# Unread full-array products in a Perceiver block's temperature network: eight ahead of its second layer in every other slot, thirteen behind its third

## What is computed

```python
qk = jnp.einsum('bhqd,bhkd->bhqk', Q, K)
scores = qk / math.sqrt(dk)
mean_sim = scores.mean(axis=(-2, -1))
max_sim = scores.max(axis=-1).mean(axis=-1)
probs = jax.nn.softmax(scores, axis=-1)
entropy_proxy = jnp.var(probs, axis=-1, ddof=1).mean(axis=-1)
feats = jnp.stack([mean_sim, max_sim, entropy_proxy], axis=-1)
hidden = jax.nn.gelu(_linear(feats, w1, b1), approximate=False)
hidden = jax.nn.gelu(_linear(hidden, w2, b2), approximate=False)
log_t = jnp.clip(_linear(hidden, w3, b3), LOG_T_MIN, LOG_T_MAX)
t = jnp.exp(log_t)[..., None]
attn = jax.nn.softmax(qk / (2.0 * t), axis=-1)
out = jnp.einsum('bhqk,bhkd->bhqd', attn, V)
```

## Time and profile before

| | |
|---|---|
| runs | 1214.53, 1217.95 and 1223.5 us, median 1217.95 |
| span of the profiled execution | 1213.1 us |
| TensorE products busy | 1101.5 us (91%) |
| VectorE, ScalarE, GpSimd busy | 812.4, 765.5 and 406.0 us |
| mean granted clock of TensorE | 0.897 |

### The profile page before, as it was taken

How to read it: one execution, slowest core, us unless ns; L and a number is a source line. 1 busy time by engine, 2 the same in 40 slices (tenths; PEclk the granted TensorE clock), 3 DMA queues, 4 the chain that set the end, 5 groups by cost and what they waited for, 6 DMA issues and landing times.

```text
span 1213.1 us, 39205 instructions
## 1 busy us (share of the span) xinstructions
PE 1101.5 (91%) x14964; PEld 892.8 (74%) x14964; DVE 812.4 (67%) x2128; ACT 765.5 (63%) x1547; POOL 406.0 (33%) x420
## 2 busy tenths in 40 slices
PE   3867799999999999999999999999999999999864
PEld 3535587878888787878878797878787887867743
DVE  4467667566776776677777776577667777578245
ACT  2434576776766676767766776667767676766521
POOL 2268352223232331433232332333143233331223
PEclk9968798987979897989999898989889898989787
DMA  4610010201010111102010111102020100000000
GB/s 132 193 29 27 23 37 4 61 11 42 19 44 21 36 29 28 37 2 54 11 45 20 37 29 29 36 4 61 2 54 11 45 20 19 3 2 6 8 2 9
DMA packets 46812, 38.85 MB, mean 32 GB/s; under 512 B 14576, under 2 KB 46000, under 8 KB 46640
## 3 DMA queue, kind: packets, MB, share of 16 engines
q1 hardware_dynamic: 46640, 36.41, 11.1%
HBM read 34.30 MB, written 2.10 MB: 30 GB/s over the span
## 4 chain that ended last, share of the span: by engine, by line
PE 75%; DVE 12%; issue 5%; ACT 4%; DMA 2%; POOL 1%; SPq 1%; DVEq 0%; ACTq 0%; POOLq 0%
PE pjp L665 14%; PE s1p L704 14%; PE s2p L735 13%; PE pjp L658 12%; PE pvp L752 8%; DVE est L1392 3%; DVE negm L1386 2%; PE tlp L848 2%; PE tlp L866 1%; PE tlp L787 1%; ACT ering L1045 1%; PE tlp L842 1%; PE s2p L725 1%; PE s2p L645 1%; PE tlp L809 1%
## 5 line engine op out<-in xcount | busy, mean ns | idle before, releaser
L1386 DVE TENSOR_REDUCE negm<-s1p 128x1 f32<-128x400 f32 (+1 forms) x512 | 289.8, 566 | 199.1 <-PE s1p L704 196.6
L1045 ACT ACTIVATE ering<-s1p,negm 128x400 f32<-128x400 f32 (+1 forms) x512 | 303.8, 597 | 118.6 <-DVE negm L1386 112.2
L1056 ACT ACTIVATE pring<-s2p 128x512 f32<-128x512 f32 x427 | 240.8, 565 | 148.1 <-PE s2p L735 145.1
L704 PE MATMUL s1p<-kt,qbd 32*128 32x400 f32 (+1 forms) x1024 | 305.2, 608 | 28.1 <-ACT ering L1045 26.1
L1392 DVE BATCH_NORM_STATS2 est<-ering 128x6 f32<-128x400 f32 (+1 forms) x512 | 290.7, 568 | 19.6 <-ACT ering L1045 19.6
L735 PE MATMUL s2p<-q2bd,kt 32*128 32x128 f32 (+1 forms) x3192 | 244.6, 285 | 0.0
L735 PEld LDWEIGHTS s2p<-q2bd,kt 32*128 32x128 f32 (+1 forms) x3192 | 233.3, 194 | 5.8
L658 PE MATMUL pjp<-cr,wkv 128*128 128x256 f32 (+1 forms) x1344 | 192.4, 295 | 29.7 <-DVE vt L1358 19.2
L1264 POOL TENSOR_TENSOR cr<-stage,cr 128x512 fp32r<-128x512 f32 (+1 forms) x112 | 132.1, 1180 | 234.3 <-ACT cr L1036 234.3
L658 PEld LDWEIGHTS pjp<-cr,wkv 128*128 128x128 f32 x1344 | 171.8, 198 | 45.5 <-issue 29.1
L665 PE MATMUL pjp<-wkv,cr 128*128 128x256 f32 (+1 forms) x1200 | 195.7, 318 | 10.0 <-ACT kt L1018 9.8
(11 more groups left out here) (278 smaller groups left out, 1033.1 us busy)
## 6 DMA issues: line engine op xcount, KB each, us to landing
stage<-in_ctx SPq DMA_DIRECT2D x96, 256.0 KB, 3.0
qbd<-q_dram SPq DMA_DIRECT2D x128, 8.0 KB, 1.8
stage<-in_ctx SPq DMA_DIRECT2D x16, 65.0 KB, 2.5
vt<-in_x SPq DMA_DIRECT2D x1, 1024.0 KB, 6.8
q_dram<-late SPq DMA_DIRECT2D x1, 1024.0 KB, 4.6
late<-in_x SPq DMA_DIRECT2D x7, 128.0 KB, 2.3
out_y<-late SPq DMA_DIRECT2D x7, 128.0 KB, 1.8
late<-in_gate SPq DMA_DIRECT2D x1, 768.0 KB, 4.9
```

The lines of the kernel that those rows point to most:

```text
L704: nc.tensor.matmul(s1p[u % 3][:, 0:w], qbd[s.par][rows, g, :], kt[s.par][rows, g, lo:lo + w], start=True, stop=True).then_inc(s1_full, 1)
L1045: nc.scalar.activation(ering[:, u % 3, 0:w], s1p[u % 3][:, 0:w], ACT.Exp, bias=negm[s.par][:, p, c:c + 1]).then_inc(s1_exp, 1)
L1056: nc.scalar.activation(ring_place(s, v)[0:m, 0:n], s2_bank(s, v)[0:m, 0:n], ACT.Exp).then_inc(s2_exp, 1)
L1386: nc.vector.tensor_reduce(negm[s.par][:, p, ch:ch + 1], s1p[u % 3][:, 0:w], AX.X, ALU.max, negate=True).then_inc(s1_max, 1)
```

## The change

A new function, `keep_clock(s, n, at)`, issues n products of 128 by 128 by 256 on TensorE, with the projection weights as both operands and the bank of the second-score unit of step `at` (8, thus unit 24 of the batch before) as target. Nothing reads them, and no semaphore counts them: unit 24's first product starts the bank afresh. Ahead of them TensorE waits until ScalarE has read that bank (`s2_exp`), the wait that unit 24 has anyway. It is called in step 6 ahead of the network's second layer, with n = 8 in odd slots and n = 0 in even ones (the wait alone), and in step 7 behind the third layer, with n = 13 in every slot. Both calls need a batch before with second scores, so they issue nothing in slot 1 and run in slots 2 to 16: 7 x 8 + 15 x 13 = 251 products.

```diff
@@ -79,6 +79,10 @@
 MLP_AT = {5: 0, 6: 1, 7: 2}
+
+
+FILL_FOR = 8
+FILL_1, FILL_2 = {1: 8, 2: 0}, 13
 N_MLP = len(MLP_AT)
@@ -666,6 +670,14 @@
                 mm.then_inc(pj_full, 1)
+
+            def keep_clock(s, n, at):
+                s_, v = s.second(at, 0)
+                if s_.has(1, B) and not s_.drains():
+                    need(pe, s2_exp, s_.lin(S2U, v - 1 - S2U))
+                    for _ in range(n):
+                        nc.tensor.matmul(s2_bank(s_, v)[:, 0:D], wkv[:, 0, 0, 0, 0:P], wkv[:, 1, 0, 0, :], start=True,
+                                         stop=True)
 
             def temperature(s, n):
@@ -885,6 +897,7 @@
                         if step in MLP_AT and s.has(1, B):
+                            keep_clock(s, FILL_1[s.r], FILL_FOR)
                             temperature(s, MLP_AT[step])
@@ -897,6 +910,8 @@
                     if step % 2 == 1 and step in MLP_AT and s.has(1, B):
                         temperature(s, MLP_AT[step])
+                        if MLP_AT[step] == 2:
+                            keep_clock(s, FILL_2, FILL_FOR)
```

## The result

The changed kernel takes 1200.96 us (median of 4 runs, 1197.27 to 1205.8), the kernel before 1216.51 beside it: a ratio of 0.985 (95% interval 0.981 to 0.990). In a second comparison, against 19 runs of the kernel before, it was 0.989 (0.986 to 0.992). So it is faster by 1.1 to 1.5%, the way that was forecast, at half the size: 13 to 16 us where 30 were expected. All ratios leave out two slow runs, one of the experiment `quarter` (1276.81 us at a mean clock of 0.77) and one of the kernel before (1229.07 us).

The account below looks back on a forecast made before the run. TensorE, busy 91% of the span and often at half clock, was taken as the bound. Gains 36.3 - 5.5 - 5 + 4.2 = 30.0 us off 1213.1 gave 1183.1, plus 4.85 to the median: 1188 us, range 1172 to 1210.

Parts of the forecast that it names:

- only the odd slots hold: Rival, chance 0.13: even slots' first fall may move to steps 10 to 13 and cost the same; 12.4 us gained, 1205.5.
- its own case: The forecast, chance 0.60: products hold the clock in most of slots 2 to 15; 1188 us, alone spanning 1176 to 1203.
- the price of 0.21: Lower bound, from whole odd slots: 0.21 us gained per low microsecond of the whole first stretch; 0.41 of busy time was taken.
- The first low stretch: Half-clock stretch behind the network, slots 2 to 15: removal gains 2.3 us per odd slot, 2.6 per even, 36.3 in all.
- two slots that fall as before: Of the 14 slots 2 to 15, two were allowed to keep their fall: 5 us lost.
- Steps 8 and 9: Sign of being right: from first scores to the end of the twelve projection products, 5.5 us before, near 3.3 after.
- The even slots' second fall: Later low stretch in seven even slots, no product added there: up to 0.80 us a slot, 0.6 taken, 4.2 us gained.
- the array theory: On TensorE, stretches in which little of the array works, not idling alone, precede a fall of the clock.
- The thirteen: Products behind the third layer: 0.25 us overrun by 14 slots, 3.5 us; in slot 16 3.2 us, of which 2 taken.
- the eight: Products ahead of the second layer in seven odd slots: 1.11 us in a gap of 1.13, costing nothing.
- the distance to the median: The median of the runs put 4.85 us above the profiled span, so 1183.1 became 1188.
- The rule that the prediction cited: Mid-kernel drops follow long idle gaps; products would then close nothing that matters, as in the unchanged-clock rival: 1225 us, chance 0.11.

Follow-up runs that it names:

- quarter: The changed kernel with the same 251 products on 32 contraction rows in place of 128: 1220.67 us, 1.001 of the kernel before.
- Whole tiles: The changed kernel with the last context tile's projections streaming 256 columns for 66 and 128 weight columns for 65: 1184.49 us, 0.971 of the kernel before.
- trim: The changed kernel with whole last context tiles, and eleven products behind the third layer in place of thirteen: 1189.11 us, 0.973 of the kernel before.
- no16: The changed kernel with whole last context tiles, without the thirteen products in slot 16: 1186.92 us, 0.973 of the kernel before.
- the clip moved: The kernel before with VectorE's clip of the network's output moved ahead of step 8's first maximum: 1218.54 us, 1.003 of the kernel before.
- wide_only: The kernel before, without added products, with the last context tile's projections streaming whole tiles: 1212.81 us, 0.993 of the kernel before.

## Why the prediction was right, and where it was too large

The time lies in the range, the sign is right, and the mechanism is shown: full-array products in the gaps hold the clock (the changed kernel), products of a quarter of the array in the same gaps do not (quarter, even slots). The size is half of the forecast: 1200.96 and 1204.31 us are nearer to the 1205.5 of the rival "only the odd slots hold" than to 1188, at the weak end of what the prediction worked out for its own case (15 us of gain, 1203, with the price of 0.21). Each term can be looked up.

*The first low stretch, 36.3 us, less 5 us for two slots that fall as before.* It went in 13 of 14 slots and is halved in slot 2, so no slot had to be given up. Steps 8 and 9 take 3.13 to 3.15 us from slot 3 on, where 3.3 were expected. What failed is the price carried over to the whole slot. An odd slot gained 65.49 - 64.18 = 1.3 us (slot 11; 1.6 on average from 5 to 13) where 2.3 were put down. Steps 8 and 9 did gain 5.33 - 3.15 = 2.2; 0.6 went back in steps 10 and 11 to ScalarE's wait for the clip, and 0.3 to steps 6 and 7. I had excluded a limit there because "nothing behind it in the odd slots shows" one. It could not show, as TensorE came late in every slot of the kernel before; but the wait of ScalarE itself, 1.76 us, stood in the trace. The lower bound, 0.21 per low microsecond from whole odd slots, was the better price: 1.4 us.

*The even slots' second fall, 4.2 us to be had.* The sign of this term was wrong. The second fall came 1.3 to 3 us earlier, and in slots 4 to 14 it lasted 51 us in all for 41; the even slots 4 to 14 gained 1.3 us on average (68.4 to 67.1), half of what the first stretch alone should have given. This is the rival "only the odd slots hold" by another way: the first fall does not move, it goes, but the second takes its place. The row that spoke of it was in the prediction, a fall with TensorE busy throughout; I took it as a reason for the array theory and not as a bound on the sum. Whole tiles take this fall away, which is 15 us in slots 4 to 14.

*The thirteen, 0.25 us in each slot; the eight, nothing.* The eight cost nothing. The thirteen put off step 8 by 0.3 us, and trim shows that 0.24 of it is had back in steps 8 and 9. The scores that "stretch over 2.00 us" did so in part because they ran at half clock, and they are three products where the 0.94 us are four: in the changed kernel the same three take 1.27. In slot 16 they take 3.1 us at half clock, as worked out (3.2), and still no16 gained nothing without them.

*What was left out: the end.* The profiled execution before took 145.27 us from slot 15 on, that of the changed kernel 154.23, at a lower clock. From 17 us into slot 15 on there are no more projections of the context, and TensorE is busy for 125 of the changed kernel's 154 us; where the clock falls there differs from profile to profile: 42 to 62 us at half in those of the kernels with both the eight and the products behind the third layer on the whole array, 42 and 48 in those of the kernel before without and with the clip moved, and 66 in that of wide_only, which has none of the products either. So a loss of 9 us at the end can't be put down to the change from one profile of each, and it is as large as the effects in question. The span of 1213.1 us, against which the sum was made, was a good one: the device time is 1.9 to 2.0 us above the span in the runs that give both, so what I took as the distance to the median, 4.85 us, was mostly the spread of the runs; the profile of the changed kernel is of its slowest run. What in the end decides where the clock falls was not tried and stays open.

*The rule that the prediction cited.* By the Trainium skill ("TensorE: Matmul & The Clock Gate", section "Why this matters for your kernels") drops in the middle of a kernel come from long idle gaps between bursts of matmuls, and by that alone filling short ones would change nothing. This case differs: where gaps of 1.13 and 1.36 us were filled with full-array products, the first low stretch went in 13 of 14 slots; where the even slots' gap was closed with products on a quarter of the array, it stayed. So in this kernel neither the length of a gap nor its closing decides, and the rule would have given the wrong sum here.

## What to carry to other kernels

In this kernel a clock that fell in every slot could be held by full-array work in the waits, but only when every sparse spell around was looked at: with the first one held, the next fell earlier and cost more. Look first for sparse products that can be made wide at the same cost, as those of 66 columns here, and for an operation of 0.2 us that blocks another engine's queue; on top of the added products each of these gave as much again and more (1.5 to 2%; both together little beyond one), at next to no cost, and without them 0.7% and nothing. A gain at the faster clock should be priced by whole stretches that include what follows, and other engines' waits that are now hidden should be listed as what is late next.

## What the hardware showed that was not expected

- Twelve products of 128 by 128 by 66 columns take 1.53 us and twelve of 256 columns 1.66: with a new set of weights for each product, columns beyond 66 were nearly free. In the kernel with whole tiles the same step's twelve take 1.63 to 1.66 us.
- Half of a remedy can cost as much as it brings: without the eight ahead of them the thirteen products ran at half clock in the odd slots, up to 3.14 us for 1.80, and the kernel was no faster than before (1.001).
- Moving two operations of VectorE of 0.2 us each made no difference that can be measured in the kernel before (1.003, 0.999 to 1.007), and 21 us in the changed one.
